# A perceiver layer on one core: where the overfull experts' operations stand, three weighings of the drain, and who issues the last stores

## The reference

```python
x = x + cross_attention(ln(x), ctx)     # 16 heads of 64, 1601 context rows for each batch, inner layer norm with
                                        # gamma and beta, out projection, bias, times tanh(gate)
x = x + linear_attention(ln(x))         # 8 heads of 64: q softmaxed over its features, k over the sequence,
                                        # context = k^T v for each head, out projection, bias
x = x + mixture_of_experts(ln(x))       # 8 experts, 256 -> 1024 -> 256, relu, top 2 of the router's logits,
                                        # the two weights by a softmax over the two logits
```

## Time and profile before

| | |
|---|---|
| median of three runs | 929.99 us |
| the three runs | 929.99, 930.99, 921.87 us |
| the profiled execution, its own time | 927.24 us |
| its span | 925.5 us |
| TensorE busy | 894.2 us (97%) |
| TensorE's weight loads | 782.7 us (85%) |
| VectorE busy | 685.6 us (74%) |
| ScalarE busy | 542.8 us (59%) |
| GpSimd busy | 594.2 us (64%) |
| HBM traffic | 94 GB/s over the span |

### The profile page before, as it was taken

The page is one execution under the profiler, slowest core; times in us unless marked ns, Lnnn a source line. Parts: engine busy times, 40 slices in busy tenths (PEclk is TensorE's granted clock), DMA queues, the critical chain, the costliest instruction groups (busy, mean ns, idle before and its releaser), DMA issues. The chain is left out here.

```text
span 925.5 us, 17222 instructions
## 1 busy us (share of the span) xinstructions
PE 894.2 (97%) x6258; PEld 782.7 (85%) x6258; DVE 685.6 (74%) x1170; ACT 542.8 (59%) x979; POOL 594.2 (64%) x647
## 2 busy tenths in 40 slices
PE   8999999999999999999999999999889998799998
PEld 5568989898898988989898898988778677698997
DVE  6659787877978787797787879676666676867666
ACT  3647666576665766666575665657463442466663
POOL 5649578947957886795796689471000507587775
PEclk9999999999999999999999999999999999899999
DMA  5962223312322331232222122110201422366642
GB/s 166 337 222 70 60 79 81 94 52 79 92 60 80 90 89 51 78 94 63 79 76 61 47 55 67 47 38 1 69 1 62 133 80 69 107 223 228 211 143 80
DMA packets 102803, 88.24 MB, mean 95 GB/s; under 512 B 10032, under 2 KB 98112, under 8 KB 102720
## 3 DMA queue, kind: packets, MB, share of 16 engines
q1 hardware_dynamic: 101952, 85.04, 30.7%
q0 software_dynamic: 768, 2.10, 0.7%
HBM read 67.46 MB, written 19.66 MB: 94 GB/s over the span
## 5 line engine op out<-in xcount | busy, mean ns | idle before, releaser
L1676 PE MATMUL scp<-cn,pt_hi 128*128 128x258 f32 (+1 forms) x832 | 238.9, 287 | 1.5 <-ACT u_sb L900 1.5
L1677 PE MATMUL scp<-cn,pt_hi 128*128 128x256 f32 (+1 forms) x832 | 234.9, 282 | 0.0
L1678 PE MATMUL scp<-cn,pt_lo 128*128 128x258 f32 (+1 forms) x832 | 234.8, 282 | 0.0
L884 ACT ACTIVATE st<-sps 128x512 f32<-128x512 f32 (+1 forms) x208 | 123.6, 594 | 160.1 <-PE sps L1658 160.1
L1166 DVE TENSOR_TENSOR pt_lo<-st,pt_hi 128x512 fp32r<-128x512 f32 (+1 forms) x208 | 199.4, 959 | 14.9 <-ACT pt_hi L893 14.3
L1141 DVE TENSOR_TENSOR st<-st,mbc 128x512 f32<-128x512 f32 (+1 forms) x208 | 161.9, 779 | 40.0 <-ACT mbc L914 39.4
L1658 PE MATMUL sps<-qk_hi,ct_hi 128*128 128x512 f32 (+1 forms) x416 | 168.0, 404 | 3.5 <-DVE cmax L1152 2.6
L1676 PEld LDWEIGHTS scp<-cn,pt_hi 128*128 128x128 f32 (+1 forms) x832 | 156.9, 189 | 10.4 <-DVE pt_lo L1166 2.6
L1658 PE MATMUL sps<-qk_hi,ct_lo 128*128 128x512 f32 (+1 forms) x416 | 164.2, 395 | 0.0
L1677 PEld LDWEIGHTS scp<-cn,pt_hi 128*128 128x128 f32 (+1 forms) x832 | 157.2, 189 | 7.5 <-issue 0.2
L744 POOL TENSOR_TENSOR cn<-raw,zero 128x256 fp32r<-128x256 f32 (+1 forms) x104 | 83.7, 805 | 124.3 <-PE scp L1678 116.0
(11 more groups left out here) (305 smaller groups left out, 1481.6 us busy)
## 6 DMA issues: line engine op xcount, KB each, us to landing
w_raw<-W SPq DMA_DIRECT2D x22, 1024.0 KB, 7.6
raw<-ctx_t SPq DMA_DIRECT2D x96, 128.0 KB, 2.2
raw<-ctx_n SPq DMA_DIRECT2D x96, 128.0 KB, 2.1
raw<-qk_scratch SPq DMA_DIRECT2D x56, 128.0 KB, 2.0
xg_scratch<-zrow SPq DMA_DIRECT2D x32, 128.0 KB, 2.3
yg_scratch<-zrow SPq DMA_DIRECT2D x32, 128.0 KB, 2.3
qk_scratch<-stage_b SPq DMA_DIRECT2D x4, 896.0 KB, 6.3
qk_scratch<-stage_a SPq DMA_DIRECT2D x4, 896.0 KB, 6.8
```

The lines of the kernel that those rows point to most:

```text
L884: act.activation(st[0:rows(j), par, j, :], sps[0:rows(j), u % 2, :], ACT.Copy).then_inc(out_ok, 1)
L1676: pe.matmul(scp[:, t, 0:D + 2], hi, cn[0:rows(j), j, 0:D + 2], start=j == 0, stop=False)
L1677: pe.matmul(scp[:, t, 0:D], hi, cn[0:rows(j), j, D + 2:CNW], start=False, stop=False)
L1678: ins = pe.matmul(scp[:, t, 0:D + 2], lo, cn[0:rows(j), j, 0:D + 2], start=False, stop=j == SJ - 1)
```

## The change

Five edits.

1. `tri` is made while VectorE waits in the chain of token tile 3 (`n == RANKS_AT`), in the first half of expert 0.
2. `rank_over` (now `counted` and `overi` only) stands behind split 3 of expert 0's second half, `name_over` (`pick`, `unit_f`, `unit_i`) behind split 5. Ahead of unit 0's first split only `lnT_lo` is left.
3. In the drain the weighing of slot k+1 stands behind the odd tiles' steps and slot k not only for k=208, but also for each k with k % 13 equal to 2 or 5 (k=210, 213, 223, 226; at 226 nothing else stands in between).
4. TensorE's first q projections wait for one half of `xnT` at a time.
5. Of the last four stores ScalarE issues those of tiles 1 and 3, behind its last activation; SyncE issues those of 0 and 2, and waits for all.

```diff
--- before.py
+++ after.py
@@ -455,6 +455,7 @@
         comb_ok = sem("comb_ok")
         placed_ok = sem("placed_ok")
         bias_ok = sem("bias_ok")
+        stored_odd = sem("stored_odd")
 
         head_rows = (slice(0, Q), slice(Q, P))
 
@@ -710,10 +711,11 @@
                     load_x(z + 2)
                 if z < NZ - 1:
                     store_y(z)
-            for m in range(MT):
+            for m in range(0, MT, 2):
                 sp.wait_ge(placed_ok, m + 1)
                 sp.dma_start(out[P * m:P * (m + 1), :], x_sb[:, m, :]).then_inc(stored, 16)
-            sp.wait_ge(stored, 16 * MT)
+            sp.wait_ge(stored, 16 * MT // 2)
+            sp.wait_ge(stored_odd, 16 * MT // 2)
 
 
         @block.gpsimd
@@ -1065,6 +1067,9 @@
                 act.activation(y_hi[:, a, :], scp[:, b0 + a, 0:D], ACT.Copy).then_inc(y_hi_ok, 1)
                 act.wait_ge(y_lo_ok, a + 1)
                 act.activation(y_w2[:, a, :], scp[:, b0 + a, D:2 * D], ACT.Copy).then_inc(y_w2_ok, 1)
+            for m in range(1, MT, 2):
+                act.wait_ge(placed_ok, m + 1)
+                act.dma_start(out[P * m:P * (m + 1), :], x_sb[:, m, :]).then_inc(stored_odd, 16)
 
 
         @block.vector
@@ -1373,13 +1378,14 @@
                                          in1=x_sb[:, m, :], op0=ALU.mult, op1=ALU.add).then_inc(yc_ok, 1)
 
             for k in range(NSLOT, SPREAD):
-                if NSLOT < k < DRAIN:
+                late = k == NSLOT or k % SJ in (V_MR, V_U)
+                if k < DRAIN and not late:
                     weigh(0, k + 1, k + 1)
                 for m in chains_in(k, 1):
                     chain(m, k - CHAIN_AT[m])
                 if k < DRAIN:
                     slot(0, k, k)
-                if k == NSLOT:
+                if k < DRAIN and late:
                     weigh(0, k + 1, k + 1)
                 for m in chains_in(k, 0):
                     chain(m, k - CHAIN_AT[m])
@@ -1416,6 +1422,9 @@
                     choose(ROUTES_AT[n])
                 for m in SHARES_AT.get(n, ()):
                     shares(m)
+                if n == RANKS_AT:
+                    dve.wait_ge(mats_ok, 2)
+                    dve.tensor_scalar(tri[:], trio[:], 0.0, None, ALU.is_gt).then_inc(over_ok, 1)
                 if n == RANKS_AT + 1:
                     routes(0, MT - 1, "a")
             chain(MT - 1, 15)
@@ -1432,9 +1441,7 @@
                 over_done(dve.scalar_tensor_tensor(out=overe[:], in0=scp[:, MT - 1, NE:2 * NE], scalar=float(TK), in1=eidx[:],
                                                    op0=ALU.is_gt, op1=ALU.mult))
             def rank_over():
-                dve.wait_ge(mats_ok, 2)
-                over_done(dve.tensor_scalar(tri[:], trio[:], 0.0, None, ALU.is_gt))
-                after_over("tri")
+                after_over("overe")
                 over_done(dve.scalar_tensor_tensor(out=counted[:], in0=overe[:].unsqueeze(1).broadcast_to((P, NE, NE)),
                                                    scalar=0.0, in1=tri[:], op0=ALU.is_gt, op1=ALU.mult))
                 after_over("counted")
@@ -1453,6 +1460,10 @@
                 split_h(1, f)
                 if f == 1:
                     find_over()
+                elif f == 3:
+                    rank_over()
+                elif f == 5:
+                    name_over()
 
             def take_gates():
                 dve.wait_ge(gates_pe, 1)
@@ -1546,8 +1557,6 @@
                                   ALU.subtract).then_inc(y_lo_ok, 1)
 
             xt_low(0)
-            rank_over()
-            name_over()
             for z in range(NZ):
                 for f in range(FT):
                     split_z(z, f)
@@ -1606,7 +1615,7 @@
                     pe.wait_ge(pro_ql, t - GT + 1)
                 for dt in range(DT):
                     if t == 0:
-                        pe.wait_ge(pro_trc, DT)
+                        pe.wait_ge(pro_trc, dt + 1)
                     ins = pe.matmul(q_bank(t), wq_sb[:, dt, t * P:(t + 1) * P], xnT[:, dt, :],
                                     start=dt == 0, stop=dt == DT - 1)
                 ins.then_inc(pro_q, 1)
@@ -2059,7 +2068,7 @@
                 "x2 stats2 aggr2 eps2 ln2 lnT_lo logit top diff index topf oh0 oh1 cnt 1+e w0 w1 gw0 sel gw tw2")
 ROUTE_NO = number("pos_a both_a sum_a slot_a pos_b both_b sum_b slot_b")
 PAIR_NO = number("others step moved_w move kept place0 place1 weight0 weight1 index")
-OVER_NO = number("overe tri counted overi pick0 pick1 pick2 unitf unit")
+OVER_NO = number("tri overe counted overi pick0 pick1 pick2 unitf unit")
 
 
 # ---- launch ----
```

## The result

The changed kernel takes **919.55 us** (median of 14 runs, 918.29 to 921.88) beside 930.0 (median of 14, 921.87 to 931.23): a ratio of **0.9903, 95% interval 0.9888 to 0.9918**. That is 1.0% faster; 921.0 was forecast. The profiled execution of the changed kernel took 921.88, the slowest of its 14 runs.

What follows compares the result with a forecast made beforehand. TensorE, busy 97% of the span, bounds the kernel; its longest idle stretch opens unit 0. 927.24 - 8.6 (stall) + 3.95 (picks) + 1.7 (clock) - 2.4 (drain) - 0.7 (first projection) - 0.2 (stores) = 921.0 us; range 915.5 to 928.5.

Steps and rivals of the forecast that it cites:

- the first case: Expert 0's second half: first pick held once, like tri, the rest follow; 921.0 us in all, chance 0.35.
- The picks: Picks, unit_f, unit_i behind split 5, inside GpSimd's stream: cost 3.95 us (0.65 to 8.25), plus 1.7 for the clock.
- the prologue: First projection: TensorE's first three matmuls need only one half of xnT; -0.7 us (0 to 0.77).
- the stall: Start of unit 0, feed-forward: TensorE idles 6.90 us for held tri and counted, plus 1.7 for half clock; -8.6 us.
- two signs of a wrong mechanism: Picks short yet time over 919, or another wait of more than 2 us in TensorE's list.
- the drain: Weighing behind the chain: -1.2 us at k=210, -1.2 at k=213, 0 at k=223; sum -2.4.
- the stores: Kernel's end: two stores per queue, the last issued once its x_sb is done; -0.2 us, bound +0.5.
- the second rival: Expert 0's second half: picks in at each GpSimd operation's end, 1.85 us, no clock fall; 917.2 us, chance 0.32.
- tri's row: Profile row of tri, held 3.40 us by GpSimd's back-to-back stream; taken as model for the picks' 3.95 us.
- The remark that the spread may be this stall: Run-to-run spread (921.87 to 930.99) may come from how long counted is held as the two engines meet.
- The slower rival: Expert 0's second half: counted itself caught in GpSimd's stream, 12.1 us against 8.6 saved; 927.4 to 932, chance 0.07.
- margin of 0.24 us: Behind split 3 of expert 0's second half: counted expected to issue 0.24 us ahead of GpSimd's stream.

Runs made afterwards that it cites:

- over_back: Changed kernel with counted, overi, picks, unit_f, unit_i back behind lnT_lo of unit 0 (over_back_again: same kernel, rerun): 12 runs median 915.3, 12 median 924.4 us.
- wide_pool: Changed kernel with GpSimd's low-part operations for expert 1 twice as wide (128x512), half as many: 924.65 us.
- wide_gap: wide_pool with GpSimd waiting on itself between the two operations of each quarter of expert 1's weights: 915.19 us, on another chip than wide_pool.
- B: Chip of the first eight experiments; the kernel before the change took 918.9 to 923.9 us in 48 runs there, 927.0 to 931.8 in 20.
- prologue_back: Changed kernel with TensorE's first q projection waiting for both halves of xnT again: 916.5 us, 0.65 over after_again.
- after: The profiled execution of the changed kernel from the result's own runs: 921.88 us.
- names_early: Changed kernel with picks, unit_f and unit_i right behind counted and overi, behind split 3: 915.48 us, on another chip than B.
- before: The kernel without the change: median 930.0 us in A; its profiled execution, on which the prediction rested, 927.24.
- before_gap: Kernel before the change, with GpSimd waiting on itself between operations within each quarter of expert 1's weights: 920.25 us, ratio 0.9969.
- A: The set of runs behind the result, chip not recorded: changed kernel 919.55 us, kernel before 930.0.
- after_again: The changed kernel itself, unaltered, run again on B: 915.85 us, ratio to before 0.9911.
- counted_mid: Changed kernel with counted and overi behind split 4 instead of split 3 of expert 0's second half: 915.77 us.

## Why the prediction was right, and where it was not

**The number: right in part by luck.** 921.0 stood for the first case, picks held once, and that case didn't occur. The picks were priced 1.8 too high (3.95 for 2.17), and in the profiled execution the prologue came out 1.8 and the stall 0.8 the other way. Of the two signs of a wrong mechanism that the prediction gave itself, the first came true: the picks were short and the time still over 919 (919.55, and 921.88 in the profile). The second, another wait of more than 2 us, did too, though it was the one that the prediction had counted on: 3.11 ahead of L1967. What was right is the stall, what caused it, the drain and the stores.

**The stall and its cause: right.** The 6.90 us ahead of L1978 and the half clock behind them are gone. The term was 8.6 us; the two traces give 7.8 up to unit 0's seventh part: 0.41 is a new wait for h_lo ahead of it, and 0.3 of the half clock still lay behind that place in the kernel before. That a small operation there is held by GpSimd's stream is now shown by changing one thing at a time (over_back, wide_pool, wide_gap), not only read.

**The picks: the second rival.** I took 3.95 us, by tri's row. In every profile of the changed kernel and its near variants each pick came in at the next end: 2.17 to 2.5 us with unit_i (1.85 was the rival's figure; it left out that unit_i would be held as well, 0.43 to 0.45 in place of 0.17). So the time of the first case came about in another way. In the profiled execution TensorE's wait was 3.11, and the clock fell, +1.6, which the rival excluded; on B the wait was 1.8 and the clock stayed. By the terms of the case that occurred, 917.2 + 1.6 for the clock = 918.8. The profiled 921.88 is 3.1 above that: 1.8 at the prologue (below), 0.8 at the stall, 0.3 at the picks, and 0.2 in small differences.

**The prologue: mis-sized in that execution.** -0.7 was forecast. The start did come 0.5 earlier, but the clock fell at 10 us, and the same matmuls came 1.1 later. On B the edit is worth -0.65 (prologue_back). The fall at 10 us stands in 2 of the 11 profiles with the early start (after, names_early) and in none of 3 with the late start (before, before_gap, prologue_back); whether the start brings it on is open.

**The drain: right.** -1.16 and -1.20 in the traces, nothing at k=223. What I missed is that the long form can cost a fall of the clock too: 3.3 on B in place of 2.4. **The stores:** -0.2, right; ScalarE's issue takes no longer than SyncE's (0.37 and 0.34 us beside 0.35 and 0.34).

**The level.** The sum was made on an execution of 927.24, which lies at the low end of the upper group (927.0 to 931.8 on B): its hold of 3.40 and 5.25 ended at GpSimd's pause, but the median in A lies 2.8 above. The remark that the spread may be this stall was right and deserved more weight. In A 12 of 14 runs were in the upper group, so the median moved 10.5, most of it, as far as can be told, by the group that went; on B, the lower group of before (921.2) and the changed kernel (915.85) differ by 5.4, of which the drain is 3.3, the prologue 0.65, the stores 0.2, and the rest, about 1.2, stays unassigned (tri's own place is one candidate). Some of it is the clock: the lower group on B falls apart by the granted clock in a run's mean, with medians of 919.4 at 0.999 and 1.000 (10 runs), 920.8 at 0.998 (17) and 922.4 at 0.996 (19), while 11 of the 12 runs of after_again are at 1.000. At that clock the two kernels differ by 3.5, of which the drain is 2.15. The sets differ beyond the clock as well: the changed kernel's two runs at 1.000 in A took 918.3 and 918.7, on B 915.0 to 916.2. On B the moving of counted and the picks shows in the 20 of 68 runs of the upper group only.

**The slower rival** did not come, though the margin of 0.24 us that I gave it was about right: 0.30 in the profile after. It was thinner than that sounds: counted took 0.47 there in place of 0.21 in after_again, and ended 0.17 behind the start of GpSimd's stream. In the profiles of counted_mid and after_again the margin was 0.9 and 1.7.

## What to carry to other kernels

A small VectorE operation with SBUF operands that stands on the critical path should not meet a run of GpSimd operations that follow one another without a pause: it may come in at the next end, and it may be held for the whole run. Moving it works if its new place is free of them; a semaphore wait of GpSimd on itself between its operations worked as well in three kernels and costs it 0.1 us each. And where a kernel's times fall into two groups, profile one run of each before a mean is taken, since the profile at hand shows one of them only.

## What the hardware did that I had not expected

- An operation of 0.2 us waited 9.65 us for a neighbour whose operations took 0.7 to 2.3 each: nine ends lost in a row (over_back_again), seven (wide_pool, of which all 12 runs are slow), four (tri), one (over_idle), and none in the other half of over_back's runs. With a pause of about 0.1 us behind half or three quarters of GpSimd's operations no operation of VectorE waited for more than one end in the three profiles, and none of 29 runs was in the upper group. The Trainium skill ("SBUF — State Buffer", Who interferes with whom) says that the one that issues first holds the shared ports for its whole instruction and that issue order decides. The held times agree with the first half. By the second, counted, which waited while GpSimd's next operation had not begun, would come in at the first end, near 782.9, in over_back_again; it came in at 792.36, so there the trace disagrees.
- Which of two equal-looking meetings is won is open. In both profiles of over_back counted issued some 0.1 us ahead of the end of a 0.7 us operation, right behind lnT_lo; one was won and one lost. The two meetings are alike to 0.02 us: lnT_lo issued 0.02 us ahead of that GpSimd operation, and counted 0.14 ahead of its end, in both. The width of GpSimd's operations turned the picks from always won (0.70 us operations, five profiles) to lost (1.25 us operations without a pause, one profile, and 12 runs at 924 to 926). The share of runs in the upper group differs between the sets: 12 of 14, 20 of 68 and 6 of 25 runs of the kernel before. What in the phase of the two engines decides it was not tried.
- Not every operation is held. tri, counted, the picks and unit_i were, all with operands in SBUF alone. The reductions overi (0.22 us) and unit_f (0.18) and the splits, which read h from PSUM (0.41 to 0.43), took the same inside GpSimd's stream as outside it in the profile after. And VectorE's winning of an end shows on the other side: in the earlier trace rows the first of GpSimd's operations ends at 726.67 (the 726.85 of the prediction is three operations divided evenly), qe comes in there, and GpSimd's next operation takes 1.19 us in place of 0.73.
